# A four-layer network on one core: attention's result stored in a second layout, the experts' result in another layout, and the forward transforms that read them

## What is computed

```python
# layer 0, its end: attention over 320 keys, projection, residual
out = jnp.einsum('bhqk,bhkd->bhqd', attn, v)
out = out.transpose(0, 2, 1, 3).reshape(b, n, c) @ proj_w + proj_b
x1 = out.transpose(0, 2, 1).reshape(b, c, h, w) + x
# layer 1: group norm, rfft2, 32 x 32 modes through a small MLP, irfft2
xf = jnp.fft.rfft2(xp, axes=(1, 2), norm='ortho')
xm = xf[:, :m, :m]
...
# layer 1, its end: shared experts, 4 of 16 experts, residual
for e in range(NUM_EXPERTS):
    out = out + _gelu(_c1(feats, expert_w[e], expert_b[e])) * gate_w[:, e][:, None, None, None]
out1 = out + residual
# layer 2: Hartley transform, 20 x 20 modes, inverse, smoothing
x_ht = dht_2d(out1)
```

## Time and profile before

| | us |
|---|---|
| median of 3 runs | 7600.77 |
| lowest, highest | 7596.58, 7612.95 |
| the profiled execution, its own time | 7609.55 |
| its span in the profile | 7607.1 |

### The profile page before, as it was taken

The page is one execution under the profiler, slowest core; times in us unless marked ns, Lnnn a source line. Parts: engine busy times, 40 slices in busy tenths (PEclk is TensorE's granted clock), DMA queues, the critical chain, the costliest instruction groups (busy, mean ns, idle before and its releaser), DMA issues. The chain is left out here.

```text
span 7607.1 us, 120115 instructions
## 1 busy us (share of the span) xinstructions
PE 6646.3 (87%) x37246; PEld 3510.5 (46%) x37246; DVE 5727.4 (75%) x5704; ACT 3966.8 (52%) x6794; POOL 3507.3 (46%) x2382
## 2 busy tenths in 40 slices
PE   8968699999966399787999999999989999999970
PEld 7852233333245144673222222222257777777760
DVE  4653677777712287115999999999979999999975
ACT  4424466666611376104666666666555555555532
POOL 0100122222201200003777777777768888888860
PEclk9989799999977699667999999999989999999995
DMA  2253233433356423532000000000000000000016
GB/s 70 71 176 117 71 99 100 101 99 100 93 126 194 185 90 105 132 72 38 19 18 18 19 19 18 18 18 18 9 17 11 9 10 9 10 10 10 8 37 192
DMA packets 618033, 481.73 MB, mean 63 GB/s; under 512 B 248797, under 2 KB 549123, under 8 KB 609435
## 3 DMA queue, kind: packets, MB, share of 16 engines
q1 hardware_dynamic: 617819, 479.02, 23.2%
HBM read 304.91 MB, written 171.32 MB: 63 GB/s over the span
## 5 line engine op out<-in xcount | busy, mean ns | idle before, releaser
L2556 DVE TENSOR_TENSOR_SCAN spa_hs<-spa_p_d,spa_hs,spa_bx 128x483 f32<-128x483 f32 x1168 | 1476.2, 1404 | 0.0
L2282 POOL TENSOR_TENSOR spa_hc<-spa_hs,spa_cr 128x966 f32<-128x966 f32 x592 | 1224.4, 2068 | 426.8 <-DVE spa_hs L2556 410.5
L2687 POOL TENSOR_TENSOR spe_hc<-spe_hs,spe_cu 128x1024 f32<-128x1024 f32 x520 | 1216.1, 2359 | 274.6 <-DVE spe_hs L2884 274.6
L2884 DVE TENSOR_TENSOR_SCAN spe_hs<-spe_p_d,spe_bx 128x1024 f32<-128x1024 f32 x520 | 1161.0, 2274 | 6.5 <-ACT spe_p_d L2833 5.9
L1065 DVE TENSOR_REDUCE attention_nm<-attention_p_s 128x2 f32<-128x640 f32 x1024 | 789.1, 812 | 259.2 <-PE attention_p_s L922 258.1
L2761 PE MATMUL spe_p_y<-spe_idt,spe_hc 128*128 128x128 f32 x8320 | 973.3, 275 | 0.0
L2761 PEld LDWEIGHTS spe_p_y<-spe_idt,spe_hc 128*128 128x128 f32 x8320 | 951.7, 192 | 0.0
L1023 ACT ACTIVATE attention_pr<-attention_p_t 128x512 f32<-128x512 f32 x1280 | 710.6, 598 | 418.6 <-PE attention_p_t L945 287.5
L2467 ACT ACTIVATE spa_p_d<-spa_p_d,spa_av 128x483 f32<-128x483 f32 x1184 | 705.1, 634 | 409.6 <-PE spa_p_d L2339 407.6
L2833 ACT ACTIVATE spe_p_d<-spe_p_d 128x896 f32<-128x896 f32 x520 | 445.5, 899 | 795.4 <-PE spe_p_d L2746 795.2
L2542 DVE TENSOR_TENSOR spa_bx<-spa_br,spa_p_u 128x952 f32<-128x952 f32 x592 | 780.0, 1318 | 33.5 <-PE spa_p_u L2352 33.4
(11 more groups left out here) (423 smaller groups left out, 10396.9 us busy)
## 6 DMA issues: line engine op xcount, KB each, us to landing
attention_qs<-scratch_qp SPq DMA_DIRECT2D x768, 64.0 KB, 2.8
attention_rc<-scratch_den SPq DMA_DIRECT2D x128, 256.0 KB
scratch_qp<-patch_parts SPq DMA_DIRECT2D x64, 384.0 KB, 2.3
spa_xt<-scratch_x SPq DMA_DIRECT2D x148, 121.5 KB, 2.6
front_xs<-in_x_dram SPq DMA_DIRECT2D x64, 256.0 KB, 3.0
scratch_xf<-front_out SPq DMA_DIRECT2D x128, 128.0 KB, 2.5
patch_x<-scratch_xf SPq DMA_DIRECT2D x8, 2048.0 KB, 18.8
attention_xs<-in_x_dram SPq DMA_DIRECT2D x128, 128.0 KB, 4.7
```

The costliest lines, as they stand in the source:

```text
L2282: nc.gpsimd.tensor_tensor(hc[:, k % 8:k % 8 + 2, :], hs[:, k:k + 2, :], cr2[:, s % 2, :].unsqueeze(1).broadcast_to([128, 2, NA]), ALU.mult ...
L2556: nc.vector.tensor_tensor_scan(hs[:, k, v], p_d[k % 4][:, v], bx[:, k, v], 0.0 if start else hs[:, k, NA - 1:NA], ALU.mult, ALU.add).then_ ...
L2687: nc.gpsimd.tensor_tensor(hc[:, k, :, d, :].rearrange("p s d t -> p d s t"), hs[:, k % 2, d, :, :], rows, ALU.mult)\
L2884: nc.vector.tensor_tensor_scan(hs[:, k % 2, d].rearrange("p d s t -> p (d s t)"), p_d[h][:, :], bx[:, k % 2, d].rearrange("p d s t -> p (d ...
```

## The change

Attention stores each finished chunk twice: into x1 as before and into a new scratch tensor x1r of shape (H, B, C, W), by a second transfer from the same tile, right behind the first on SP and on the same semaphore, whose expected counts double. The experts store their result only as (H, B, C, W), so a tile goes out as four rows of 512 B per partition, 128 KB apart. `low_spectrum` reads a tensor with the row outermost: a partition's eight images are now 4 KB in one piece, and its rows are 128 KB apart. The residual stage reads x1 as before.

```diff
@@ -749,7 +749,7 @@
                     nc.vector.tensor_tensor(parts[:, n, 2], rest[:, n], parts[:, n, 1], ALU.subtract).then_inc(third, 1)
 
 
-def attention(nc, x, qp, kd, vdr, ident, wp, bp, den, x1, st1):
+def attention(nc, x, qp, kd, vdr, ident, wp, bp, den, x1, x1r, st1):
 
 
 
@@ -826,6 +826,7 @@
         block = st.block()
         xv = x.rearrange("b c (i q) w -> b q c i w", q=2)
         ov = x1.rearrange("b c (i q) w -> b q c i w", q=2)
+        orv = x1r.rearrange("(i q) b c w -> b q c i w", q=2)
 
         def chunks(eng, body):
 
@@ -861,8 +862,9 @@
 
             def store(c):
                 sp.wait_ge(bn_ready, c.m + 1)
-                dst = ov[c.b, c.q][:, c.rows, :] if isinstance(c.i0, int) else ov[c.b, c.q][:, 2:, :][:, bass.ds(c.i0 - 2, 4), :]
-                sp.dma_start(dst, out[:, c.u, :].rearrange("c (i w) -> c i w", w=W)).then_inc(out_stored[c.u], 16)
+                for v in (ov, orv):
+                    dst = v[c.b, c.q][:, c.rows, :] if isinstance(c.i0, int) else v[c.b, c.q][:, 2:, :][:, bass.ds(c.i0 - 2, 4), :]
+                    sp.dma_start(dst, out[:, c.u, :].rearrange("c (i w) -> c i w", w=W)).then_inc(out_stored[c.u], 16)
                 if c.u == U - 1:
                     sp.dma_start(st1[c.b, :, c.round, :], bn[:, :, :]).then_inc(bn_stored, 16)
 
@@ -906,7 +908,7 @@
             max_rows(Chunk(0, 0, 0))
             chunks(sp, body)
             for u in range(U):
-                sp.wait_ge(out_stored[u], 16 * B * NR)
+                sp.wait_ge(out_stored[u], 32 * B * NR)
             sp.wait_ge(bn_stored, 16 * B * NR)
 
         @block.tensor
@@ -1077,7 +1079,7 @@
                 dve.wait_ge(x_in[c.u], 16 * c.n + 16)
 
                 if c.old:
-                    dve.wait_ge(out_stored[c.u], 16 * c.n)
+                    dve.wait_ge(out_stored[c.u], 32 * c.n)
                     dve.wait_ge(bn_stored, 16 * c.n)
                 nc.vector.scalar_tensor_tensor(out[:, c.u, :], p_m[0:C, :], bps[:, 0:1], xs[:, c.u, :], ALU.add,
                                                ALU.add).then_inc(out_ready, 1)
@@ -1146,7 +1148,7 @@
 
 def low_spectrum(nc, name, src, c_h, c_w, low):
 
-    xv = src.rearrange("b c h w -> h (b c) w")
+    xv = src.rearrange("h b c w -> h (b c) w")
     N = B * C // G8 // 2
     with Stage(nc, name) as st:
         ch = st.sb("ch", [128, 2 * MD])
@@ -1805,7 +1807,7 @@
 def experts(nc, hr, feats, sel, wts, we, be, ws, bs, out1):
 
     NF = HW // 512
-    ov = out1.rearrange("(a p) c h w -> (p c) a (h w)", a=2)
+    ov = out1.rearrange("h (a p) c w -> (p c) a h w", a=2)
     fv = feats.rearrange("p a n -> p (a n)")
     with Stage(nc, "experts") as st:
         wes = st.sb("wes", [128, C, NE])
@@ -1851,7 +1853,7 @@
             def store(a, j, s):
 
                 sp.wait_ge(summed[NX - 1], a * N * 2 + 2 * j + s + 1)
-                sp.dma_start(ov[:, a, bass.ds((2 * j + s) * 512, 512)], os[:, s, :]).then_inc(stored[s], 16)
+                sp.dma_start(ov[:, a, bass.ds((2 * j + s) * 4, 4), :], os[:, s, :].rearrange("p (i w) -> p i w", w=W)).then_inc(stored[s], 16)
 
             for s in range(2):
                 load(s, s)
@@ -3283,9 +3285,9 @@
 
 SCRATCH = {
     "xf": (2, C, B, H // 2, W), "xs": (128, 2, 320),
-    "kd": (B, 99, 1280, BF16), "vd": (B, 128, VC), "den": (4, NH, 512), "qp": (B, 2, C, HW // 1024, 3, 512, BF16), "x1": (B, C, H, W), "st1": (B, C, 32, 6),
+    "kd": (B, 99, 1280, BF16), "vd": (B, 128, VC), "den": (4, NH, 512), "qp": (B, 2, C, HW // 1024, 3, 512, BF16), "x1": (B, C, H, W), "x1r": (H, B, C, W), "st1": (B, C, 32, 6),
     "low1": (2 * MD, B * C, MD), "modes1": (2, B, C, MD, MD), "ab1": (C, 2, B), "y1": (B * C, H, W), "feats": (128, 2, HW),
-    "fmean": (128, 2), "sel": (B, TOP, NE), "wts": (B, TOP), "out1": (B, C, H, W), "low2": (2 * MD, B * C, MD),
+    "fmean": (128, 2), "sel": (B, TOP, NE), "wts": (B, TOP), "out1": (H, B, C, W), "low2": (2 * MD, B * C, MD),
     "modes2": (2, B, C, M2 + 1, M2 + 1), "x2": (C, NCA * NA + 8), "ys": (C, NCA * NF), "xf2": (C, NCA * NF), "steady": (128 * ST,), "ye": (C, LF),
 }
 
@@ -3314,9 +3316,9 @@
     gated_frequencies(nc, *of("x c_h c_w ident fg1 fg2 c_k c_f xf"))
     patches_and_queries(nc, *of("xf sr1 sr2 srb wq bq ident xs qp"))
     keys_and_values(nc, *of("xs ident ln wk bk part_rows wv dwv kd vd"))
-    attention(nc, *of("x qp kd vd ident wp bp den x1 st1"))
-
-    low_spectrum(nc, "low1", *of("x1 c_h32 c_w32 low1"))
+    attention(nc, *of("x qp kd vd ident wp bp den x1 x1r st1"))
+
+    low_spectrum(nc, "low1", *of("x1r c_h32 c_w32 low1"))
     fourier_mlp(nc, *of("low1 st1 groups8 gn1 sign afno1 afno2 afnob modes1 ab1"))
     low_inverse(nc, "inv1", t["modes1"], MD, *of("c_k32 c_m32"), t["y1"].rearrange("(b c) h w -> h b c w", b=B))
     with nc.sbuf_tensor("hr", [128, 2, HW], F32) as hr:
```

## The result

The changed kernel takes 7658.6 us (median of 6 runs, 7640 to 7664) beside 7607.3 us for the kernel before (6 runs): ratio 1.0062, interval 1.0046 to 1.0079, so 35 to 60 us slower. The forecast was 7633 in a range of 7600 to 7690, slower with a chance of 0.76. The direction held; of its three terms the second store came out too small, the gain of the loads too large, and the loss in the experts all but absent.

A forecast was written before the change was run, and what follows sets the result against it. PE looked like the bound in all four stages, with SP's in-order issue queue within 0.6 to 0.8 us of its pace in attention. The terms +40 - 20 + 12 = +32 us gave 7633, range 7600 to 7690.

The forecast's parts named there:

- the second store: Attention: 128 more issues on SP add 102 us before the tail, less 66 us of slack; taken as +40 us.
- the gain of the loads: Low1 and low2: loads in 4 KB pieces land 0.5 us earlier; together -20 us, ends 0 and -34.
- the loss in the experts: Experts: storing four rows of 512 B per partition costs +12 us, ends 0 and 22.
- if all slack can be used ... I take 40: Attention: 102 - 66 = 36 us if all slack is used; 40 taken because the slack isn't evenly spread.
- The lower end: Attention: SP finds the denominators landed sooner, 14 us could come back, so the second store costs 22 us.
- Rivals 1 and 2: Attention: 1, SP stays just under PE's pace, 17 us, chance 0.14; 2, second store free, kernel faster, chance 0.07.
- rival 3: Attention: the whole issue time is paid, 102 us, perhaps through query loads all taking 3.9 us; 7695, chance 0.13.
- 0.5 us earlier covers them, so 13 us go: Low1 and low2: steady waits of 0.22 and 0.29 us per load vanish when loads land 0.5 us earlier, 13 us.
- that share, which I had put at 6 us: Low1 and low2: half of the 12 us clock difference in PE's busy time comes back, since PE has fewer gaps.
- Rival 4: Low transforms and experts: the size of the pieces buys and costs nothing, leaving +40 alone; 7641, chance 0.12.
- half the bytes, half the difference: 0.35 us: Experts: two 512 KB stores differ 3.3 to 2.6 us by piece size; half that on each of 32 pairs, 11 us.
- the experts' stage doesn't move: Experts: the stage was to grow 10 to 13 us; no movement was named as a sign the forecast is wrong.

The follow-up runs named there:

- e3: The changed kernel with attention's second store issued behind the transfer of the inverted denominators, before SP waits for it; ratio 0.9997 to the kernel before.
- e11: The kernel before plus only attention's second store, placed behind the transfer of the row maxima in SP's list; ratio 1.0093 to the kernel before.
- e6: The changed kernel with the second store in the wait for the denominators and four load buffers in both transforms; ratio 0.9960 to the kernel before.
- e7: The kernel before with four load buffers instead of two in both transforms, old layouts everywhere; ratio 0.9955 to the kernel before.
- e10: The kernel before with its only attention store in the wait for the denominators and four load buffers in the transforms; 7561.4 us, ratio 0.9928.
- e1: The kernel before plus only attention's second store, right behind the first, to a tensor nothing reads; ratio 1.0054 to the kernel before.
- e2: The kernel before with only the experts' store and low2's loads in the new layout; ratio 0.9992 to the kernel before.

## Why the prediction was right or wrong

**The second store: right in its mechanism, +40 instead of +53.** The sum was 102 us of added SP time less 66 us of slack. The first number held: in the chunk shown the second store delays the next issue by 0.84 us (1645.02 to 1645.86) and the first by 0.92, as before. The step that was mis-sized is "if all slack can be used ... I take 40". 51 of the 66 us were used (66.4 to 15.3), and 102 - 51 = 51 us; measured were 53 between the profiled executions of before and changed, 49 to 53 against the mean of three. Since SP works in order, this agreement is bookkeeping: it says where SP's time went, and what shows the cause is e3, where the same issues at another place cost next to nothing. The lower end, 14 us back from the denominators' wait, did not come (150.3 to 148.3). Rivals 1 and 2 (17 us and nothing) and rival 3 (102 us, the whole issue time) are out, and so is the reason of the last: one query load takes 375 ns to issue in the median, before and after.

**Which wait is next.** I named the row maxima first and POOL second. The trace and e11 show POOL: PE's wait for the row maxima rose from 1.1 to 9.1 us, its wait for POOL's output from 14.9 to 46.5. Together that is 40 us; PE's holes grew by 42. In the prediction's list of what is queued behind the store, the denominators were there but I gave them no path to PE. They are the last in SP's list, so they collect its whole delay.

**The other place for the store: not seen.** The prediction counted the wait for the denominators as latency inside the chain (1.26 us a chunk) and did not ask what could be done in it. E3 puts the same store there, and attention takes 2 to 5 us more than with one store (e6 and e3 against 1290.1), within the scatter.

**The transforms' loads: -20 forecast, about -12 in the profiled executions, none clear of noise in the totals.** Landing was right (3.5 forecast, 3.6 measured). The step that failed is "0.5 us earlier covers them, so 13 us go". The longest wait in the steady part before was 0.61 us in low1 and 0.81 in low2, so 0.5 less would have covered nearly all of them if nothing else had moved. In the changed kernel there are fewer waits, 10 instead of 15 in low1 and 7 instead of 14 in low2, but some are longer than any before, up to 1.16 and 1.07 us: the median landing fell in both stages, the slowest did not in both (4.5 and 5.0 us before, 5.0 and 4.8 changed, the first loads left out). The waits fell by 0.7 and 4.2 us, 5 of the 13.

From PE's first product to its last, low1 took 108.5 us on average over seven executions with the old layout and two buffers, and 105.1 over three with the new; low2 121.1 over six and 112.3 over four. That is -3.4 and -8.8, with values up to 12 us from these means. About half of it, 1.0 and 5.0 us, is PE's busy time, which is the clock's: that share, which I had put at 6 us, was right in size. Whether the shorter waits cause the better clock is not settled: e3's low2 had the short landings, a clock of 0.77 and 124.7 us. Without gaps it was 0.94 to 0.95 in three of the four stages of e7 and e6, and 0.94 in both of e10. The totals don't confirm the -12: the changed kernel is not faster than e1, which lacks both layouts (1.0062 and 1.0054), and e2's -6 us has an interval that holds 0. Rival 4, the layouts buying and costing nothing, gives 7641, nearer the measured 7658.6 than my 7633; its premise holds for the experts' store, and for the loads it does not (3.6 us instead of 4.0).

**The experts: +12 forecast, about +1 measured.** The step that failed is "half the bytes, half the difference: 0.35 us". The pair it was taken from (3.3 and 2.6 us) belongs to two other stages with other traffic, so the layout was not their only difference. Durations from issue to landing (min/median/max), before, then changed:

```profile
DMA to landing us min/median/max: 2.0/2.4/3.3
```

```profile
DMA to landing us min/median/max: 2.3/2.5/3.3
```

The shortest grew by 0.3 us, the longest not at all. In the earlier trace rows DVE is released 3.3 us after an issue, at the long end; its wait is 16.2 us in all, 16.0 before. The mechanism of a loop through the store was not tested, since nothing lengthened it. The prediction named "the experts' stage doesn't move" among the signs that it is wrong, and that sign came: this term is refuted.

**The size of the pieces and the pitch of the rows.** The experts' store lands as soon in 512 B pieces as in 2 KB (2.5 and 2.4 us), the loads of the transforms don't (4.0 us in 512 B pieces, 3.6 in 4 KB). The Trainium skill, "DMA: Bandwidth & Descriptors", section "Specifications", has pieces from 512 B up at line rate; the store agrees with it, the loads less so. In the changed kernel no load or store of the new layout, at a pitch of 128 KB, lands later than its counterpart by more than 0.1 us in the median. The Trainium skill's figures on the pitch ("Latency and other measured facts") begin at 512 KiB, and there its 207 GB/s is close to the 214 that it calls full, so by them too nothing was to be feared at 128 KB; the prediction read that row as a slowdown.

**The sum.** 53 - 12 + 1 = +42, against 47 between the profiled executions and an interval of 35 to 60. The errors of the terms partly cancel (+13, +8 and -11), so it is in part luck that +32 came as near as it did. The rest is in stages that nothing touched: the MLP and the inverse behind low1 were 2 and 3 us longer in the changed kernel's profile, within what they differ by over all thirteen executions (57.5 to 60.6 and 131.7 to 137.1 us).

## What to carry to other kernels

A queue that issues transfers is an engine: list its issues and waits for one turn of the loop and compare the sum with the pace of the busiest engine before adding to it; a wait that is pure latency inside that list is a nearly free place for an issue that nobody is waiting for (2 to 5 us here, 53 right behind the first store). A mean wait says little about what a faster transfer will remove: here one more pair of buffers took away 13 and 27 us where a better layout took away 3 and 9, and made the layout nearly indifferent. The second layout cost its issues here, not its bytes, with the DMA engines 0.43 busy.

## What was not expected of the hardware

The four-row store, 128 KB between rows, costs 406 ns to issue instead of 356 and lands after 2.5 us instead of 2.4, which is within what other executions show (2.3 to 2.5, and 2.2 to 2.4). A store of 64 pieces takes 537 ns to issue whether it carries 4 or 32 KB, and one of 256 pieces and 128 KB 634. The granted clock in the two transforms, which run the same instructions, lies between 0.77 and 0.94 from one execution to the next with two load buffers, and low2 has the lower one in every kernel with the old layout (0.79 to 0.85 against 0.88 to 0.94 in low1); what differs between the two stages was not found.
